# A residual sum kept in DRAM: scattering the first stage's rows as they are made, instead of gathering them in the next stage

## The reference, cut to what matters

```python
x = x + tanh(g_xattn[0]) * routed(layernorm(x), ids, ctx)      # each token to one of 4 experts by its id;
                                                               # y = (silu(h @ c.T) * (h @ c.T)) @ c with c = ctx[e]
x = x + tanh(g_ffn[0]) * mx_ffn(layernorm(x), w_gate, w_up, w_down)   # block-quantised gated MLP, 512 -> 2048 -> 512
x = x + tanh(g_xattn[1]) * attention(layernorm(x), ctx, ctx)
x = x + tanh(g_ffn[1]) * moe(layernorm(x), ...)                # 64 experts, top 6, and a shared one
return x
```

## Time and profile before

| | us |
|---|---|
| median of three runs | 1103.11 (1102.46 to 1104.67) |
| the profiled execution | 1105.25 |
| its span in the trace | 1103.5 |

### The profile page before, as it was taken

One profiled execution on the slowest core, in us unless ns is written; L12 is line 12 of the kernel. 1 busy time (PEld: TensorE's weight loads), 2 busy tenths in 40 slices (PEclk: granted clock), 3 DMA queues, 4 the chain that ended last, 5 costly groups with the idle time before them and its releaser, 6 DMA issues. The chain is left out here.

```text
span 1103.5 us, 13632 instructions
## 1 busy us (share of the span) xinstructions
PE 978.7 (89%) x4378; PEld 475.3 (43%) x4400; DVE 672.1 (61%) x1238; ACT 401.2 (36%) x797; POOL 641.9 (58%) x554
## 2 busy tenths in 40 slices
PE   5999999388888897699999998998999999999960
PEld 4455554134444443344444454333555555555530
DVE  7888998677888884577777776893222222222220
ACT  4444544233444342566666643222211111111100
POOL 4666663778999885676767730336354544554530
PEclk9999999699999998899999989998999999999995
DMA  7556331401111000600005122138999999999547
GB/s 260 160 173 208 121 130 65 67 10 20 20 20 20 10 2 1 224 25 20 20 20 184 60 78 75 58 124 277 330 345 343 343 343 347 342 341 343 123 57 152
DMA packets 65171, 161.71 MB, mean 147 GB/s; under 512 B 9888, under 2 KB 10032, under 8 KB 64592
## 3 DMA queue, kind: packets, MB, share of 16 engines
q1 hardware_dynamic: 49488, 120.74, 30.9%
q0 software_dynamic: 15616, 40.12, 16.4%
HBM read 129.54 MB, written 35.48 MB: 150 GB/s over the span
## 5 line engine op out<-in xcount | busy, mean ns | idle before, releaser
L1080 POOL TENSOR_TENSOR ARENA<-ARENA 128x512 f32<-128x512 f32 x128 | 133.6, 1065 | 59.6 <-DVE ARENA L1106 59.6
L803 PE MATMUL PS<-SLAB,ARENA 128*128 128x512 bf16 x497 | 116.2, 382 | 8.0 <-DVE ARENA L642 5.3
L1361 POOL DMA_INDIRECT out<-ARENA,idx x32 | 46.0, 1437 | 131.6 <-DVE ARENA L1499 126.8
L1726 ACT ACTIVATE ARENA<-PS 96x192 f32<-96x192 f32 x64 | 20.9, 327 | 228.8 <-PE PS L1619 228.8
L1499 DVE COPY ARENA<-PS 96x512 f32<-96x512 f32 x64 | 41.1, 682 | 93.8 <-PE PS L1638 93.8
L1200 ACT ACTIVATE ARENA<-PS,ARENA 128x512 f32<-128x512 f32 x128 | 86.9, 683 | 22.9 <-DVE ARENA L1100 19.7
L1619 PE MATMUL PS<-SLAB,ARENA 128*96 128x384 f32 x240 | 83.5, 502 | 0.0
L1161 PE MATMUL PS<-ARENA 64*128 64x512 f32 x256 | 75.5, 669 | 8.3 <-DVE ARENA L1094 4.9
L1100 DVE TENSOR_REDUCE ARENA<-PS 128x2 f32<-128x1024 f32 x64 | 78.2, 1221 | 7.3 <-PE PS L1161 7.1
L372 POOL TENSOR_TENSOR XNT<-XNT,ARENA 128x1536 f32<-128x1536 f32 x16 | 45.6, 2848 | 58.6 <-DVE ARENA L545 58.6
L803 PEld LDWEIGHTS PS<-SLAB,ARENA 128*128 128x128 bf16 x512 | 48.9, 98 | 67.1 <-issue 12.5
(11 more groups left out here) (247 smaller groups left out, 1882.2 us busy)
## 6 DMA issues: line engine op xcount, KB each, us to landing
SLAB<-in_L_ffn_w_gate SPq DMA_DIRECT2D x30, 384.0 KB, 19.3
SLAB<-in_L_ffn_w_up SPq DMA_DIRECT2D x30, 384.0 KB, 20.4
X<-in_L_ffn_w_down SPq DMA_DIRECT2D x14, 768.0 KB, 17.5
SLAB<-in_L_ffn_w_down SPq DMA_DIRECT2D x10, 768.0 KB, 17.6
CT<-in_L_ffn_w_gate SPq DMA_DIRECT2D x16, 384.0 KB, 19.3
CT<-in_L_ffn_w_up SPq DMA_DIRECT2D x16, 384.0 KB, 20.5
slot_out<-ARENA SPq DMA_DIRECT2D x19, 256.0 KB, 2.0
X<-in_ctx SPq DMA_DIRECT2D x4, 1024.0 KB, 8.9
```

The lines of the kernel that those rows point to most:

```text
L803: last = pe.matmul(bank(b), QT[:, par, k * P:(k + 1) * P], w[:, k, c * D:(c + 1) * D], start=(k == 0), stop=(k == KD - 1))
L1080: last = pool.tensor_tensor(prob[:, s % 4, h, :], prob[:, s % 4, h, :], rec[:, s % 4, h:h + 1].to_broadcast([P, D]), ALU.mult)
```

## The change

The rows of a finished slot no longer go to `slot_out`. A DRAM tensor `x_sum` holds 2048 rows for the tokens and 19 x 128 spare rows. ACT issues four transfers of 1 MB that copy x from DRAM to DRAM into it, ahead of its ninth copy of the context. DVE works out `target`: the token of a place if it has one, else a spare row of its own. POOL scatters each slot's `ysb` by `target` and adds it in the transfer. SP waits for all 19 scatters and loads X tile by tile with 16 ordinary transfers. SP's 19 stores and its 8 loads of x, and POOL's 16 gathers of the MLP stage, are gone.

```diff
-    slot_out = nc.dram_tensor("slot_out", [SLOTS * P, D], F32, kind="Internal").ap()
+    x_sum = nc.dram_tensor("x_sum", [T + SLOTS * P, D], F32, kind="Internal").ap()
...
-        picks = SLAB[:, 10240:10240 + NT * SLOTS].bitcast(BF16).rearrange("p (i n j) -> p i n j", n=2, j=SLOTS)
-        at_tile = SLAB[:, 11008:11008 + NT * SLOTS // 2].bitcast(BF16).rearrange("p (i j) -> p i j", j=SLOTS)
+        picks = SLAB[:, 10240:10240 + 3 * NT * SLOTS // 2].bitcast(BF16).rearrange("p (i n j) -> p i n j", n=3, j=SLOTS)
+        at_tile = picks[:, :, 2, :]
...
@@ SP
-                def store_y(j):
-                    sp.wait_ge(y_out, j + 1)
-                    sp.dma_start(slot_out_v[:, j, :], ysb[:, j % 2, :]).then_inc(y_stored[j % 2], 16)
...
                 for j in range(SLOTS):
                     if j in TILED and tile_at(j) + 2 < NT:
                         load_w(tile_at(j) + 2)
-                    if 1 <= j <= 8:
-                        need(sp, c_turned, NT)
-                        sp.dma_start(X[:, 2 * j - 2:2 * j, :], x_v[:, 2 * j - 2:2 * j, :]).then_inc(x_in, 16)
-                    if j:
-                        store_y(j - 1)
-                store_y(SLOTS - 1)
+                sp.wait_ge(y_stored[0], 16 * ((SLOTS + 1) // 2))
+                sp.wait_ge(y_stored[1], 16 * (SLOTS // 2))
+                for i in range(NT):
+                    need(sp, yg_in[i % 4], 16 * (i // 4))
+                    sp.dma_start(X[:, i, :], x_sum_v[:, i, :]).then_inc(yg_in[i % 4], 16)
@@ POOL
+                def scatter(j):
+                    if j == 0:
+                        pool.wait_ge(target_ready, 1)
+                        pool.wait_ge(x_in, 64)
+                    pool.wait_ge(y_out, j + 1)
+                    pool.indirect_dma_start(x_sum, bass.IndirectOffsetOnAxis(ap=target[:, j:j + 1], axis=0),
+                                            ysb[:, j % 2, :], None, compute_op=ALU.add).then_inc(y_stored[j % 2], 16)
                 for j in range(SLOTS):
                     if j in TILED:
                         normal(tile_at(j) + 1)
+                    if j:
+                        scatter(j - 1)
                     if j + 3 < SLOTS:
                         deviation(j + 3)
                     if j + HR < SLOTS:
                         gather(j + HR)
                 for n in REST[1:]:
                     normal(n)
+                scatter(SLOTS - 1)
...
-                def gather_x(i):
-
-                    need(pool, yg_in[i % 4], 16 * (i // 4))
-                    pool.indirect_dma_start(X[:, i, :], None, slot_out, bass.IndirectOffsetOnAxis(ap=slot[:, i:i + 1], axis=0),
-                                            compute_op=ALU.add).then_inc(yg_in[i % 4], 16)
-
-                pool.wait_ge(x_in, 16 * 8)
-                pool.wait_ge(y_stored[0], 16 * ((SLOTS + 1) // 2))
-                pool.wait_ge(y_stored[1], 16 * (SLOTS // 2))
-                for i in range(4):
-                    gather_x(i)
...
-                    if i + 6 < NT:
-                        gather_x(i + 6)
@@ DVE, ahead of picks_ready and behind token_ready
+                own.link(dve.scalar_tensor_tensor(out=pads[:, 0, :], in0=iota_f[:, 0:SLOTS], scalar=float(P),
+                                                  in1=own_p[:, 0:1].to_broadcast([P, SLOTS]), op0=ALU.mult, op1=ALU.add))
+                own.link(dve.tensor_scalar(pads[:, 0, :], pads[:, 0, :], float(T), None, ALU.add))
...
+                own.link(dve.tensor_tensor(pads[:, 1, :], pads[:, 0, :], bank(3)[:, 2 * SLOTS:3 * SLOTS], ALU.mult))
+                own.link(dve.tensor_tensor(pads[:, 0, :], pads[:, 0, :], pads[:, 1, :], ALU.subtract))
+                dve.tensor_tensor(target, pads[:, 0, :], token, ALU.add).then_inc(target_ready, 1)
@@ PE
-                    last = pe.matmul(bank(3)[:, 0:2 * SLOTS], at_row[:, i, :], picks[:, i].rearrange("p n j -> p (n j)"),
+                    last = pe.matmul(bank(3)[:, 0:3 * SLOTS], at_row[:, i, :], picks[:, i].rearrange("p n j -> p (n j)"),
@@ ACT
                 for t in range(NT):
+                    if t == 8:
+                        for b in range(B):
+                            act.dma_start(x_sum[b * S:(b + 1) * S, :], x_rows[b * S:(b + 1) * S, :]).then_inc(x_in, 16)
                     act.wait_ge(c_turned, t + 1)
```

More of the change, by code:

```diff
@@ L171, in build @@
         hot_ready, counted = sem("hot_ready"), sem("counted")
-        whose_ready, picks_ready, found, token_ready = (
-            sem(n) for n in ("whose_ready", "picks_ready", "found", "token_ready"))
+        whose_ready, picks_ready, found, token_ready, target_ready = (
+            sem(n) for n in ("whose_ready", "picks_ready", "found", "token_ready", "target_ready"))
         h_in = [sem(f"h_in{r}") for r in range(5)]
@@ L204, in build @@
         token = arena(SLOTS, I32)
+        target = arena(SLOTS, I32)
+        pads = arena(2 * SLOTS).rearrange("p (n j) -> p n j", n=2)
         idi = arena(P, I32)
@@ L230, in build @@
         x_rows = x.rearrange("b s d -> (b s) d")
-        slot_out_v = slot_out.rearrange("(j p) d -> p j d", p=P)
+        x_sum_v = x_sum[0:T, :].rearrange("(i p) d -> p i d", p=P)
         def blocks(a, n=BLK):
@@ L423, in back_i @@
                                        ALU.mult).then_inc(iq_ready, 1)
-                def gather_x(i):
-                    need(pool, yg_in[i % 4], 16 * (i // 4))
-                    pool.indirect_dma_start(X[:, i, :], None, slot_out, bass.IndirectOffsetOnAxis(ap=slot[:, i:i + 1], axis=0),
-                                            compute_op=ALU.add).then_inc(yg_in[i % 4], 16)
-                pool.wait_ge(x_in, 16 * 8)
-                pool.wait_ge(y_stored[0], 16 * ((SLOTS + 1) // 2))
-                pool.wait_ge(y_stored[1], 16 * (SLOTS // 2))
-                for i in range(4):
-                    gather_x(i)
                 deviation_x(0, 1)
                 deviation_x(1, 1)
-                gather_x(4)
                 normal_h(0)
@@ L441, in _ @@
                 deviation_x(2, 2)
-                gather_x(5)
                 normal_h(1)
```

## The result

The changed kernel takes 1110.42 us (median of four runs, 1109.27 to 1112.40), the kernel before 1103.68 (four runs beside it). The ratio is 1.0063, with an interval of 1.0046 to 1.0081: slower by some 7 us, where 2.4 us faster was predicted, and 1.4 us above the upper end of the range. The profiled execution took 1110.51 us, its span is 1108.4.

A forecast was written before the change was run, and what follows sets the result against it. No engine bounds both stages: PE is busiest in the first, POOL in the MLP. Terms -9.9 + 4.5 + 0 + 2.5 + 0.5 = -2.4 gave about 1100.7 us against 1103.11; range 1094 to 1109.

The forecast's parts named there:

- 1. The gathers go: -9.9: MLP stage: removing POOL's 16 gathers saves 9.9 us, with a gain of 7 to 11.
- tile 6's 1.3: Filling of the MLP pipeline: 1.3 us counted of PE's 1.62 us wait behind tile 6's gather.
- 2. The scatters: +4.5: First stage: 19 scatters on POOL ahead of deviations, mostly absorbed, cost 4.5 us, ends 0 and +9.
- third case: First stage: deviation beginning later against DVE's passes, its last operation at 61.76, ending at 63.14 with DVE's line 551.
- Rival C: First stage becomes POOL's, scatters with blocking lasting over 2.5 us; +7, about 1110 us; chance 0.22.
- 3. SP's stores and loads: 0: First stage: SP's 19 stores and 8 loads go, not waited for; 0, to -0.5 us.
- 4. The start: +2.5: Start: routing operations 0.5 us, first statistics some 2 later as copy shares DMA engines; +2.5, ends +0.5 and +7.
- rival D: Start: the copy holds it, +7 us instead of 2.5; sum +2, about 1105 us; chance 0.10.
- 5. The hand-over: +0.5: First stage to MLP: last scatter lands, X loads, fourth tile's statistics begin; +0.5 us, -0.8 to +1.5.
- forecast 4 to 6: Hand-over: SP's first load of X comes 4 to 6 us after the last scatter's start.

The follow-up runs named there:

- number 8: Changed kernel without the copy of x, its scatters plain writes that don't add; 1094.27 us, ratio 0.9903 to the kernel before.
- number 5: Changed kernel with the copy in 2 KB rows, issued by SP behind the third weight tile; 1100.70 us, ratio 0.9962.
- number 10: Changed kernel with SP's tiny loads of gates and gam issued first and the copy in 8 KB pieces; 1100.45 us, ratio 0.9952.
- number 7: Changed kernel with the copy in 8 KB pieces, same place and queue; 1110.87 us (one run).
- numbers 1 and 9: 1: kernel before plus only the copy, 1116.14 us. 9: changed kernel with SP's tiny loads of gates and gam issued first, 1106.36 us.
- number 12: Kernel before plus only one of the four 1 MB copies of x; 1108.35 us (one run).

## Why the prediction was wrong, step by step

**1. The gathers go: -9.9. Right.** First to last addition to X: 194.35 before, 185.39 after, -8.96; filling the pipeline gave another 1.0, for which the step had counted tile 6's 1.3. The additions of line 662, after, come every 12.5 or 13.2 us, as the earlier trace rows had it for tiles without gathers:

```profile
300.12 0.74 DVE L662 SCALAR_TENSOR_TENSOR X<-PS,tgate,X 128x512 f32<-128x512 f32 x1
313.35 0.74 DVE L662 SCALAR_TENSOR_TENSOR X<-PS,tgate,X 128x512 f32<-128x512 f32 x1
325.81 0.75 DVE L662 SCALAR_TENSOR_TENSOR X<-PS,tgate,X 128x512 f32<-128x512 f32 x1
```

and PE's wait of 1.71 in the earlier trace rows is down to 0.19:

```profile
302.25 0.62 PE L815 MATMUL PS<-ident_b,ARENA 128*128 128x128 bf16 x8 [0.19 <-POOL ARENA L431]
```

**2. The scatters: +4.5. Too high for this kernel (+1.85).** The duration was right, 1.6 in the estimate and this in the trace (ns, min/median/max):

```profile
L386 POOL DMA_INDIRECT x_sum<-ARENA x19: 1624/1638/2899, 60.8 to 213.9; - x19
```

So was the main idea, that a scatter fills time in which POOL would stand blocked. The scatters of slots 0 and 1, the deviations behind them, and PE:

```profile
60.82 1.67 POOL L386 DMA_INDIRECT x_sum<-ARENA  x1 [0.16 <-issue]
63.75 1.38 POOL L364 TENSOR_SCALAR ARENA<-ARENA 128x1 f32<-128x1 f32 x1
64.13 0.95 DVE L552 TENSOR_SCALAR ARENA<-XNT 128x1536 int16<-128x1536 int16 x1
...
70.82 1.63 POOL L386 DMA_INDIRECT x_sum<-ARENA  x1 [0.16 <-issue]
73.74 1.38 POOL L364 TENSOR_SCALAR ARENA<-ARENA 128x1 f32<-128x1 f32 x1
74.11 0.95 DVE L552 TENSOR_SCALAR ARENA<-XNT 128x1536 int16<-128x1536 int16 x1
76.02 0.66 PE L731 MATMUL PS<-ident,ARENA 128*128 128x128 f32 x4 [0.66 <-ACT ARENA L861]
```

Both deviations end with DVE's line 552 (65.13 and 75.12 against 65.08 and 75.06), the "third case" of the step. The stall at slot 3 was 0.66 instead of 2.1, slot 7 had 0.65, and slot 15, which the step didn't name, had 1.25 against 0.57 before: together 2.0, about the 1.85. In other kernels the pace did cost more: +3.4 without the copy (number 8), +4.55 in number 5 (with a weight wait in it). Part of this step's cost may have been hidden by the late start, but that isn't shown: number 10, only 4.2 us late, has +1.3, and number 7, over 13 us late by ACT's wait, has +3.3. Rival C didn't come: the longest scatter took 2.90 us, 1.3 more than the shortest, and not the 2.5 more that the prediction worked out from the Trainium skill's figures (SBUF — State Buffer, "SBUF: two separate sides").

**3. SP's stores and loads: 0. Nothing contradicts it**; no run tested it alone.

**4. The start: +2.5, and this is the step that failed.** It was +13.3, beyond even the +7 of its upper end and of rival D. The step saw the place and the means (full DMA engines, 4 MB more, gathers that wait behind large pieces) and mis-sized the wait. Rival D had named it, with a 7 that no row gave. Three things were wrong in it.

- *The share.* I let the gathers and the copy share the engines by bytes, so that a gather of 256 KB would lose some 2 us to a copy of 4 MB. By the packet counts they take turns by piece. A piece of the copy holds an engine for 2.4 to 2.9 us at 64 KB (0.608 x 64 / 16 and 0.954 x 64 / 21), for 0.37 at 8 KB (0.638 x 64 / 109, as 365 - 256 = 109 of number 7's packets are pieces of 8 KB). A gather makes some 5 packets on each engine (before, from 55 to 165 us, thirteen gathers made 1033 packets on 16 engines), and each waits for one piece. That is 1.9 us at 8 KB; at 64 KB an engine has only four pieces, so the gather waits for nearly the whole copy, 9.7 to 11.6 us (estimates). Measured were 3.6 and 11.4 at the statistics, 0.5 of each the routing's, and 3.3 with 2 KB. So at the small sizes some 1 to 2.5 us come on top; I take them for the shared bandwidth, the part that I had counted, but no run shows it apart. Same bytes, same place, 8.1 us apart between 64 and 2 KB. The Trainium skill states turns of this kind (DMA: Bandwidth & Descriptors, "Queues, rings and completion order"): each engine goes round the queue rows and changes only at the end of a packet. I had weighed another section of that page, that queues of different issuers share the engines, which was true and gave no size. The traces agree with the rule at one packet for each turn with pieces of 64 and of 8 KB (38, 34, 30 and 122, 121, 122), where a packet is one piece, however long; with 2 KB they don't show it (531 to 127).
- *A wait that I didn't look for.* SP's loads of `gates` and `gam` aren't waited for in the trace before, so they appear in none of its rows. They are three loads of 128 pieces of a few bytes, issued behind the weights, and one piece a turn made them land at 34.8 instead of before 20.75. Alone that wait costs as much as the gathers' (number 7). Beside the late gathers it adds 0.8 us of waiting and some 0.8 for line 894 and its two followers, which had been done in the gathers' shadow.
- *The clock, for 0.4 at most.* From the first normalisation to slot 0's scaling it is 18.96 us, against 18.58 before. PE's first four transposes are no part of that, with 1.09 us at a granted 0.50 in both. The first products behind them took 6.19 us at 0.59 (from 38.45) against 5.82 at 0.63 (from 25.52).

The three together: 11.4 to the statistics, 1.5 from there to the first normalisation (3.92 against 2.39) and 0.4 to slot 0, which is the 13.3.

**5. The hand-over: +0.5. Right.** At the step's own mark, the fourth tile's statistics, it was +1.1 (224.99 against 208.75, less the 15.15 of slot 18), inside the -0.8 to +1.5, and the filling of the pipeline took that back. The last scatter, SP's loads and the first statistics:

```profile
213.92 1.65 POOL L386 DMA_INDIRECT x_sum<-ARENA  x1 [0.30 <-issue]
218.98 12.85 SPq L334 DMA_DIRECT2D X<-x_sum  x15
221.72 0.69 DVE L620 BATCH_NORM_STATS2 ARENA<-X 128x6 f32<-128x512 f32 x1 [2.16 <-DMA X<-x_sum]
```

SP begins 5.06 us after the scatter's start, inside the forecast 4 to 6.

With the measured start in it, the sum of the prediction becomes -9.9 + 4.5 + 13.3 + 0.5 = +8.4. The two profiled executions, on which the sum is made, differ by 5.3. Of the 3.1 between, step 2 is 2.65, and the rest is small terms of both signs. So the start alone turns the sign, and it isn't all of the error. Number 5, without the start's delay, came to -0.38%, or -4.2 us. With only the routing's 0.5 for the start the sum of the prediction is -4.4.

What stays open: why the first gathers of numbers 1 and 9 landed 1.2 to 2.2 us earlier than the changed kernel's beyond the routing's part, why the gathers get fewer than one packet a turn beside pieces of 2 KB, and whether the 3.4 us of pace in number 8 can be had back by another order on POOL.

## What to carry to other kernels

Judge an added bulk transfer by the length of its pieces beside those of the transfers on the critical path, not by its bytes: cut it to their size, or issue it where nothing short is in flight, and look at what is queued behind it. List every load that is in flight at that time, those too that nobody waits for in the old trace, since a delay of ten microseconds finds them; and after a cure look again, because a second wait of the same cause can lie beside the first and give back nothing until both are gone. An operation put ahead of one that stands blocked anyway is nearly free (19 scatters of 1.64 us, 31 us in all, cost this kernel's stage 1.85), and putting it off can hold back the buffer that it sets free.

## What the runs showed of the hardware

- DMA engines gave three busy queues the same number of packets, whatever their bytes: 122 of the copy, 121 of the gathers and 122 of SP's in the same 4 us, with 0.89, 0.39 and 0.00 MB (pieces of 8 KB); 38, 34 and 30 with pieces of 64 KB; but 531 of the copy and 127 of the gathers with pieces of 2 KB.
- 1 MB from DRAM to DRAM, contiguous on both sides, went in 16 pieces of 64 KB, each 2.4 to 2.9 us on its engine, and 16 tiny packets (32 packets and 1.05 MB on q10 in number 12).
- A scatter of 128 rows of 2 KB takes POOL 1.04 us as a write and 1.64 with an add in the transfer, and lands 5.0 to 7.1 us after its issue with it.
- Loads of 4 to 8 bytes for each of 128 partitions landed at 34.8 beside a copy in 64 KB pieces and at 34.6 beside one in 8 KB pieces, against 20.75 at the latest without it.
